# A cross-attention kernel on one Trainium2 core: the stack's k loads behind the first half's rows, the output tile lifted by ACT, the residual added by Pool

## The reference

```python
q = heads(x @ w_q)                                   # B=16, S=256, 20 heads, 16
out_text = softmax(q @ heads(text @ w_k).T / 4) @ heads(text @ w_v)
out_ip   = softmax(q @ heads(ip @ w_k_ip).T / 4 + mask) @ heads(ip @ w_v_ip)
out = (out_text + out_ip) @ w_out + b_out + x
```

## Time and profile before

| | |
|---|---|
| time, median of 3 runs | 558.0 us (553.15 to 563.45) |
| the profiled execution | 556.4 us, of it the span from first to last instruction 554.6 us |
| busy, share of the span: PE | 481.5 us, 87% |
| DVE | 384.9 us, 69% |
| ACT | 280.3 us, 51% |
| POOL | 127.9 us, 23% |
| mean granted TensorE clock | 0.972 of full speed |

### The profile page before, as it was taken

How to read it: one execution, slowest core, us unless ns; L and a number is a source line. 1 busy time by engine, 2 the same in 40 slices (tenths; PEclk the granted TensorE clock), 3 DMA queues, 4 the chain that set the end, 5 groups by cost and what they waited for, 6 DMA issues and landing times.

```text
span 554.6 us, 12517 instructions
## 1 busy us (share of the span) xinstructions
PE 481.5 (87%) x4304; PEld 323.7 (58%) x4304; DVE 384.9 (69%) x706; ACT 280.3 (51%) x355; POOL 127.9 (23%) x205
## 2 busy tenths in 40 slices
PE   3979899999999586799799889897987988989985
PEld 2868687887887463455455555554554555555542
DVE  2739425325325256899779989897997999999932
ACT  3633335344344013666556666565664666666671
POOL 6014000000000000432323332331332433332341
PEclk9989999999999787999979999999998999999999
DMA  8978888888788935672681762672754654763211
GB/s 271 362 266 149 259 298 273 309 268 293 272 261 270 345 120 179 200 243 74 204 261 33 247 221 89 234 233 79 235 170 154 219 154 144 245 204 103 72 52 47
DMA packets 94195, 112.49 MB, mean 203 GB/s; under 512 B 14304, under 2 KB 72992, under 8 KB 94144
## 3 DMA queue, kind: packets, MB, share of 16 engines
q1 hardware_dynamic: 93296, 109.89, 60.6%
q0 software_dynamic: 848, 1.90, 1.9%
HBM read 73.17 MB, written 38.63 MB: 202 GB/s over the span
## 4 chain that ended last, share of the span: by engine, by line
PE 48%; DMA 15%; issue 11%; SPq 10%; DVE 9%; ACT 4%; POOL 3%; DVEq 0%; ACTq 0%; POOLq 0%
PE pv L730 10%; DMA max_rows<-row_buf 10%; PE score_t L716 5%; PE pj L739 4%; PE score_q L666 3%; ACT probs L471 3%; SPq L278 3%; PE score_t L625 3%; PE score_t L626 3%; PE score_t L627 3%; SPq L285 2%; PE pj L625 2%; DMA q_stack<-max_rows 2%; PE pj L627 2%; PE pj L626 2%
## 5 line engine op out<-in xcount | busy, mean ns | idle before, releaser
L534 DVE TENSOR_REDUCE max_cols<-score_q 128x4 fp32r<-128x992 f32 x160 | 187.1, 1170 | 46.4 <-PE score_q L666 41.1
L471 ACT ACTIVATE probs<-score_t 128x1024 f32<-128x1024 f32 x160 | 163.4, 1021 | 72.0 <-PE score_t L716 71.9
L730 PE MATMUL pv<-probs,v_cur 128*32 128x256 f32 x1920 | 124.5, 394 | 0.6 <-ACT probs L471 0.6
L387 POOL TENSOR_TENSOR o_turned<-o_turned,inv_cols 128x256 f32<-128x256 f32 x80 | 49.8, 622 | 179.7 <-DVE inv_cols L589 179.7
L716 PE MATMUL score_t<-q_stack,k_stack 64*128 64x256 f32 x440 | 56.5, 335 | 29.4 <-ACT probs L471 17.6
L730 PEld LDWEIGHTS pv<-probs,v_cur 128*32 128x32 f32 x1920 | 55.3, 111 | 41.1 <-issue 4.6
L462 ACT ACTIVATE o_all<-pv 128x512 f32<-128x512 f32 x80 | 47.8, 598 | 60.7 <-PE pv L730 60.7
L716 PEld LDWEIGHTS score_t<-q_stack,k_stack 64*128 64x128 f32 x440 | 33.8, 189 | 74.8 <-ACT probs L471 37.7
L739 PE MATMUL pj<-wo_sb,o_all 128*128 128x320 f32 x192 | 69.0, 468 | 2.9 <-DVE o_all L594 2.2
L381 POOL TENSOR_TENSOR x_all<-x_all,bias_sb 128x640 f32<-128x640 f32 x16 | 24.9, 1554 | 192.5 <-DMA x_all<-in_x 192.5
L586 DVE STREAM_TRANSPOSE o_turned<-o_all 128x512 f32<-128x512 f32 x80 | 56.1, 702 | 11.9 <-ACT o_all L462 11.9
(11 more groups left out here) (134 smaller groups left out, 719.5 us busy)
## 6 DMA issues: line engine op xcount, KB each, us to landing
q_stack<-q_parts SPq DMA_DIRECT2D x33, 320.0 KB, 4.5
k_stack<-k_parts SPq DMA_DIRECT2D x33, 320.0 KB, 5.6
v_rows<-v_out SPq DMA_DIRECT2D x32, 320.0 KB, 2.4
v_cur<-v_rows SPq DMA_DIRECT2D x16, 640.0 KB
o_all<-in_ctxT SPq DMA_DIRECT2D x16, 512.0 KB, 5.2
q_parts<-qk_out SPq DMA_DIRECT2D x32, 256.0 KB, 2.5
k_parts<-qk_out SPq DMA_DIRECT2D x32, 248.0 KB, 4.7
x_all<-in_x SPq DMA_DIRECT2D x16, 320.0 KB, 3.3
```

Of the source, the lines that this page charges most:

```text
L387: pool.tensor_tensor(out, out, inv_cols[:, k, :].unsqueeze(2).broadcast_to([P, 2 * S // 32, DH]), ALU.mult).then_inc(scaled, 1)
L471: nc.scalar.activation(probs[:, slot(u, p), :], score_t[:, :], ACT.Exp, scale=SCALE)\
L534: nc.vector.tensor_reduce(out=max_cols[:, h, :, at:at + 4:2].rearrange("p t e -> p e t"), in_=both[:, :, :, 0:TEXT], op=ALU.max, axis=AX.X ...
L730: last = mm(pv[32 * t:32 * t + 32, at:at + S], values_of(u, kind, 4 * k + t), probs[:, slot(u, 2 * k + t // 2), a:a + S], start=kind != 1, ...
```

## The change

Three things. In SP's turn the order becomes: `load_rows(b, 1)`; the three loads of q and the mask of batch b+2; `load_values(b+1)`; `store_out(b-2)`; `load_residual(b)`; `store_rows(b+1, 0)`; `load_rows(b+1, 0)`; the three loads of k of batch b+2; `store_rows(b+1, 1)`. `finish` leaves DVE: ACT copies `pj` to `out_sb` (`lift`), for row tile 0 of batch b-1 behind the exp of p = 7, for row tile 1 of batch b-2 behind the exp and the evacuation of p = 0, and PE's next row tile waits for that. Pool adds `x_res` to both row tiles at once (`add_residual`, at the head of its turn, for batch b-2), and adds the bias of batch b-1 between its quads 1 and 2 (`add_bias`); `store_out` waits for Pool's addition. Behind the last turn Pool adds the residual of batch 14, the bias of 15 and the residual of 15.

```diff
@@ -143,7 +143,7 @@
         st_ready, exp_done = sem("st_ready"), sem("exp_done")
         pv_ready, o_evac = sem("pv_ready"), sem("o_evac")
         turned, inv_done, scaled = sem("turned"), sem("inv_done"), sem("scaled")
-        biased = sem("biased")
+        biased, out_evac = sem("biased"), sem("out_evac")
         o_added = sem("o_added")
         o_ready = sem("o_ready")
         out_ready, out_done, out_stored = sem("out_ready"), sem("out_done"), sem("out_stored")
@@ -319,20 +319,27 @@
                 ahead, next_, first = t.there(2), t.there(1), isinstance(b, int) and b == 0
                 if not first:
                     load_rows(t, 1)
+                if ahead:
+                    scored(t, 0)
+                    for j in range(3):
+                        load_q(t.to(2), j)
+                    load_aux(t.to(2))
+                if next_:
+                    need(sp, pv_ready, QUADS * b)
+                    load_values(b + 1, 1 - u)
                 if t.there(-2):
                     store_out(b - 2)
                 load_residual(b, u)
-                if ahead:
-                    scored(t, 0)
-                    load_stack(t.to(2))
                 if next_:
-                    need(sp, pv_ready, QUADS * b)
-                    load_values(b + 1, 1 - u)
                     store_rows(b + 1, 0)
                     load_rows(t.to(1), 0)
+                if ahead:
+                    for j in range(3):
+                        load_k(t.to(2), j)
+                if next_:
                     store_rows(b + 1, 1)
             def store_out(b):
-                need(sp, out_done, OT * (b + 1))
+                need(sp, out_done, b + 1)
                 sp.dma_start(rows(out[bass.ds(b * S, S), :]), out_sb[:, :, :]).then_inc(out_stored, 16)
             batches(sp, batch, tail=False)
             for b in (B - 2, B - 1):
@@ -375,12 +382,21 @@
                 pool.dma_start(aux_of[:, e, 0:MASKS, :], mask_out).then_inc(aux_stored, 16)
             pool.wait_ge(w_low, 3)
             pool.memset(o_norm_t[:, :, :, :], 0.0).then_inc(preset, 1)
-            def normalise(t):
-                b, u = t.b, t.u
+            def add_residual(b, u):
+                pool.wait_ge(out_evac, OT * (b + 1))
+                pool.tensor_tensor(out_sb[:, :, :], out_sb[:, :, :], x_res[:, u, :, :], ALU.add).then_inc(out_done, 1)
+            def add_bias(b, u):
                 pool.wait_ge(xr_loaded[u], 8 * (b - u) + 16)
                 pool.tensor_tensor(x_res[:, u, :, :], x_res[:, u, :, :],
                                    bias_sb[:, :].unsqueeze(1).broadcast_to([P, OT, D]), ALU.add).then_inc(biased, 1)
+            def normalise(t):
+                b, u = t.b, t.u
+                if t.there(-2):
+                    pool.wait_ge(biased, b - 1)
+                    add_residual(b - 2, u)
                 for k in range(QUADS):
+                    if k == 2 and t.there(-1):
+                        add_bias(b - 1, 1 - u)
                     n = QUADS * b + k
                     out = turned_blocks(k)[:, :, 0:DH]
                     pool.wait_ge(inv_done, n + 1)
@@ -394,6 +410,11 @@
             pool.wait_ge(preset, 8)
             pool.wait_ge(ld["small"], 32)
             batches(pool, normalise, tail=False)
+            pool.wait_ge(biased, B - 1)
+            add_residual(B - 2, 0)
+            add_bias(B - 1, 1)
+            pool.wait_ge(biased, B)
+            add_residual(B - 1, 1)
         @block.scalar
         def _(act):
             def high(dst, src, loaded, value):
@@ -461,6 +482,11 @@
                 need(act, turned, n + 1 - QUADS)
                 nc.scalar.activation(o_raw[:, k, :], pv[:, :], ACT.Copy)\
                     .then_inc(o_evac, 1)
+            def lift(b, t):
+                act.wait_ge(out_ready, OT * b + t + 1)
+                if t == 0:
+                    need(act, out_stored, 16 * b)
+                nc.scalar.activation(out_sb[:, t, :], pj[:, 0:D], ACT.Copy).then_inc(out_evac, 1)
             def batch(t):
                 b, u = t.b, t.u
                 for p in range(PAIRS):
@@ -473,7 +499,11 @@
                     for k, off in EVACUATE.get(p, ()):
                         if t.there(off):
                             evacuate(b + off, (u + off) % 2, k)
+                    for m, off in LIFT.get(p, ()):
+                        if t.there(off):
+                            lift(b + off, m)
             batches(act, batch)
+            lift(B - 1, OT - 1)
         @block.vector
         def _(dve):
             steps = [0]
@@ -593,13 +623,6 @@
                     need(dve, out_ready, OT * (b - 1))
                 nc.vector.transpose(o_norm[:, u, c, :].rearrange("p (j n) -> p j n", n=32),
                                     o_norm_t[:, c, :, :]).then_inc(o_ready, 1)
-            def finish(b, u, t):
-                dve.wait_ge(out_ready, OT * b + t + 1)
-                if t == 0:
-                    need(dve, out_stored, 16 * b)
-                    dve.wait_ge(biased, b + 1)
-                nc.vector.tensor_tensor(out_sb[:, t, :], pj[:, 0:D], x_res[:, u, t, :], ALU.add)\
-                    .then_inc(out_done, 1)
             def batch(t):
                 b, u = t.b, t.u
                 for p in range(PAIRS):
@@ -611,13 +634,9 @@
                     for k, off in INVERT.get(p, ()):
                         if t.there(off):
                             invert(b + off, k)
-                    for m, off in FINISH.get(p, ()):
-                        if t.there(off):
-                            finish(b + off, (u + off) % 2, m)
                     if p % HALF == HALF - 1 and t.there(1) and t.there():
                         turn(b + 1, p // HALF)
             batches(dve, batch)
-            finish(B - 1, 1, OT - 1)
         @block.tensor
         def _(pe):
             mm = nc.tensor.matmul
@@ -735,7 +754,7 @@
                 if t == 0:
                     pe.wait_ge(o_ready, OC * b + c + 1)
                 if c == 0:
-                    need(pe, out_done, OT * b + t)
+                    need(pe, out_evac, OT * b + t)
                 last = mm(pj[:, 0:D], o_norm[:, u, c, t * P:t * P + P], wo_sb[:, c, :],
                           start=c == 0, stop=c == OC - 1)
                 if c == OC - 1:
@@ -763,7 +782,7 @@
 INVERT = {3: [(0, 0)], 5: [(1, 0)], 7: [(2, 0)], 9: [(3, 0)], 1: [(4, -1)]}
 TURN_BACK = {8: [(0, 0)], 2: [(1, -1)], 4: [(2, -1)]}
 OUT = {3: [(0, 0), (0, 1)], 5: [(0, 2)], 7: [(1, 0), (1, 1)], 9: [(1, 2)]}
-FINISH = {6: [(0, -1)], 0: [(1, -2)]}
+LIFT = {7: [(0, -1)], 0: [(1, -2)]}
 FIRST_SCORES = {3: [0, 1], 4: [2], 5: [3], 6: [4], 7: [5, 6], 8: [7], 9: [8, 9]}
 _INS = ["x", "xT", "ctxT", "ctx_sp", "bbox", "wq", "wk", "wv", "wk_ip", "wv_ip", "wo", "bias",
         "grid", "kaux", "vones"]
```

## The result

The changed kernel took 596.6 us (median of 4 runs, 590.2 to 606.4) against 558.2 us: slower by a factor of 1.068 (95% interval 1.054 to 1.082). The slowest of the four ran in a slower state of the chip, and the factor leaves it out. I had forecast 576 us, slower, with a range that ended at 590. The sign was right and the size half of what came. The profiled execution took 596.8 us, its span 595.0; against that of before this is 40.4 us more, where my sum said 19.4.

The account below looks back on a forecast made before the run. The prediction took a chain alternating between PE and ACT as the bound, with late rows of half 0 on top. Its terms, -13.7 + 0.6 + 22.5 + 5.6 + 4.4 = +19.4 us on 556.4, gave 576 us; range 563 to 590.

Parts of the forecast that it names:

- The floor of a turn: Turns 1 to 14: an alternating PE and ACT chain of 19.7 us, 21.6 us a turn with the change's other parts.
- the lifts: ACT's copies delay PE 1.5 us at p = 7 (22.5 us in all) and 0.4 us at p = 0 (5.6 us).
- The wait for half 0's rows goes: Start of turns 1 to 14: PE no longer waits for these rows; gain 13.7 us.
- k is just hidden: Start of a turn: k lands just before PE wants it at s + 21.85; it costs only +0.6 us, in turn 0.
- s + 14: SP's queue: half 0's store lands 14 us after the turn's start s, where it landed at s + 17.3.
- rival 3: Turn starts: k lands later than wanted, each of 13 turns grows 0.4 to 1.1 us, 581 to 591 us; 14 in 100.
- The end: Behind the last turn: batch 14's store 2.8 us later, Pool's last addition 1.6 us more; together 4.4 us.
- Turn 0: First turn, without lifts: k comes late and adds 0.6 us to its 22.0, between 0 and +1.5.
- DVE and Pool at 0: In the turns: DVE's two lost additions and Pool's added work change the time by 0.
- Rival 4: The new pause at p = 7 lowers PE's clock; 14 us if in 7 turns, 590 us; 10 in 100.

Follow-up runs that it names:

- e9: e5 with one edit: the lifts stand at p = 7 and p = 0 behind exp and evacuation, as in the changed kernel; 571.3 us, ratio 1.025.
- e5: e4 with the values, the store of out and the residual moved behind half 0's rows; 545.3 us, ratio 0.972.
- e2: The changed kernel with k loaded with q again, in front of the values, and two buffers of `out_sb`; 573.9 us, ratio 1.029.
- e1: The kernel before with only the three loads of k moved behind half 0's rows; 574.5 us, ratio 1.028.
- e4: e2 with the lifts put between exp and evacuation, at p = 6 and p = 0; 559.8 us, ratio 0.999.
- e12: e6 with the two rounds of the loop over turns written out; 541.5 us, ratio 0.973.
- e7: The changed kernel with one edit: the values are loaded last of all, behind k; 580.6 us, ratio 1.035.
- e8: The kernel before with the store and load of half 0's rows issued by ACT instead of SP; 567.9 us, ratio 1.010.
- e6: The kernel before with one edit: the values are loaded behind half 0's rows; 544.6 us, ratio 0.972.

## Why the prediction was too low

Point by point, in its own order:

- **The floor of a turn and the lifts: right.** Forecast 21.6 us, measured 21.5 (turn 5). At p = 7 1.53 us against 1.5 in turn 5, the longest of the fifteen; the others are 1.34 to 1.47. At p = 0 0.33 (2.03 us between `key_scores` of p = 1 and p = 2, 1.70 before) against 0.4. All together 26.0 us against 28.1. The lift's own 0.44 us is the smaller part of it: its place behind an exp is what costs. e9 against e5 prices it without any other wait: 26 to 30 us. e2 shows it alone.
- **The wait for half 0's rows goes: right.** PE waits for them nowhere in the turns of the changed kernel. The longer turn alone isn't enough: in e2 4.2 us of it are left.
- **"k is just hidden": the step that failed.** It rested on half 0's store landing at s + 14, and this on two readings. I took the start of the burst of loads, s + 3.2, from turn 5 of before, a turn that had itself begun late: half 1's store left at s + 0.3 there. In a turn that begins in time it leaves at s + 1.3, and the burst begins at s + 4.5. And I scaled the time of the burst by its bytes, 3.5 us less than 14 for 0.96 MB. It was 12.9 us, so k's leaving took off 1.1 us; against e2, which has the changed order with k left in, 1.3 us in turn 5. The first misreading is 1.3 us, the second 2.4, and together they put the store's landing at s + 17.5 and not at s + 13.8 (I had taken 14), and k at s + 24.3. Behind the landing my terms hold: 2.1 us to the third load's issue and 4.5 to 5.6 us of loading give s + 24.1 to 25.2.

  The price is the step from p = 0 to p = 1 of turns 1, 3, 4, 6, 8, 10, 12, 13 and 14, beyond its usual 2.1 us: 19.7 us together. Of this 11.9 us are the waits for k, and most of the rest is a lowered clock in the same step. In turn 8 about 1.8 of the 2.3 us are not k's: e5 loses as much in this step behind the loop's pause, with no wait for k. Behind the wait of turn 6 the clock costs another 1.4 us. That leaves 19.3 us to k and the clock behind it, of the 21.0 us by which the sum missed.

  This was rival 3, with 14 in 100 and at most 15 us; mechanism right, the size and the chance too small. What I hadn't seen is the alternation (e1). Each of the five turns that were not held up (2, 5, 7, 9, 11) was followed by one that waits for k; of the held-up ones whose next turn exists, some hid their own k and some (3, 12, 13) did not. So nine of the fourteen turns lose 1.2 to 3.4 us.
- **The end: right in kind, too small.** 9.2 us against 6.3 (4.4 and the lifts of turn 15). The lifts took 1.9 as forecast, the wait for batch 14's store 2.5 and Pool's last addition 1.6, again as forecast (2.8 and 1.6). The rest is the clock, which I had left out: it fell at p = 2 of turn 15 (1.6 us), and it was 0.74 in the last 19 us, where six projections took 3.57 instead of 1.88 us.
- **Turn 0:** forecast +0.6, measured -0.7 us.
- **DVE and Pool at 0: right** (e4 against before: 0.999; turns of e5 and e12: 19.67 and 19.76 us).
- **Rival 4, a lower clock by the pause at p = 7:** e9 refutes it for this pause alone. In the changed kernel the clock did fall, and not only behind long waits:

```profile
301.71 0.68 PE L685 MATMUL score_q<-stack 64*128 64x256 f32 x4 [1.32 <-DMA stack<-k_parts]
302.32 2.79 PE L749 MATMUL pv<-probs,v_cur 128*32 128x256 f32 x24
...
396.57 0.50 PE L735 MATMUL score_t<-stack 64*128 64x256 f32 x4 [3.33 <-issue]
...
443.75 0.50 PE L685 MATMUL score_q<-stack 64*128 64x256 f32 x4 [1.54 <-DMA stack<-k_parts]
...
560.25 0.50 PE L735 MATMUL score_t<-q_stack,k_stack 64*128 64x256 f32 x4 [1.53 <-ACT probs L497]
560.68 2.25 PE L749 MATMUL pv<-probs,v_cur 128*32 128x256 f32 x24
```

It fell behind a wait for k of 1.32 us in turn 4, but not behind one of 1.54 us in turn 10. It fell behind the loop's pause in turn 8. In turn 15, with no k in play, it fell behind a wait of 1.53 us for an exp; e9 has the same wait there and kept its clock. What decides, and whether the pauses at p = 7 have a share in it, no run shows.

Reckoned together: -13.7 + 0.6 + 28.1 + 4.4 was forecast. On top came 19.3 us of k and its clock, 2.9 us at the end and 2.9 us at the loop's second round (a pause 1.1 us longer and 1.8 us of clock behind it); 1.3 us fell away at turn 0 and 2 us at the lifts. That makes 41 us, and 40.4 were measured.

What stays open: why k's 0.96 MB are worth so little of the burst's time. By turn 5 the store landed 9.5 us after q's first load with 2.0 MB in front (e7), 10.2 with 2.2 (e5), 12.9 with 2.6 and 14.2 with 3.6 (e2): more bytes, more time, but not in proportion.

## What to carry to other kernels

A copy that lasts 0.44 us costs 1.4 to 1.5 us if it stands behind an instruction that its reader also waits behind: put it where its engine waits anyway (p = 6, in front of the evacuation, free). When a wait on a small transfer is to go, look for the largest transfer in front of it that has time, and move that one: one load of values moved was worth 2.8%, moving k cost 2.8%. Take arrival times from a turn that is not itself held up by the wait that you remove.

## What the hardware showed that I had not expected

- A 32 KB store lands 2.3 to 2.4 us after its issue when nothing is under way (half 1's store in most turns), and 4.2 to 8.4 us after it when 2.2 to 3.6 MB of loads went out just ahead of it (e5, before, e8), also from another engine's queue (e8).
- The granted clock fell to its lower level behind pauses of PE of 1.27, 1.32 and 1.53 us (turns 14, 4 and 15 of the changed kernel) and stayed at full speed behind others of 1.0 to 1.5 us (its turns 1, 3, 10, 12, 13), behind all those of p = 7 in e9, and behind 2.24 us in the kernel before (turn 8). The length of the pause doesn't tell them apart.
- The jump back to the loop's start stops PE for 2.1 to 3.9 us (e2, e5), once in each kernel with the loop. With the clock behind it turns 7 and 8 lose 3 us (e6) to 7 us (e5) together, and nothing when the loop is written out (e12).
